# Row maxima of the second attention: the two heads of a step reduced by one VectorE instruction instead of two

## What is computed

```python
x = layernorm(x + differential_attention(x))   # 16 heads of width 8
x = layernorm(x + fp4_ffn(x))                   # 352 hidden
x = layernorm(x + causal_attention(x))          # 16 query heads, 4 key heads, width 64, rotary
x = layernorm(x + top1_experts(x))              # 8 experts, 512 hidden
```

```python
logits = einsum('bqhgd,bkhd->bhgqk', rotary(q), rotary(k)) / sqrt(64)
logits = where(causal, logits, -1e30)
w = softmax(logits)                 # exp(l - max l) / sum
out = einsum('bhgqk,bkhd->bqhgd', w, v) @ Wo + bo
```

## Time and profile before

| | |
|---|---|
| median of 3 runs | 1437.1 us (1436.81 to 1442.52) |
| the profiled execution | 1440.72 us, of which the span that the profile shows is 1438.9 us |
| TensorE busy | 1171.1 us (81%) |
| VectorE busy | 796.9 us (55%) |
| ScalarE busy | 646.9 us (45%) |
| GpSimd busy | 466.6 us (32%) |
| mean granted TensorE clock | 0.863 of full speed |

### The profile page before, as it was taken

One profiled execution on the slowest core, in us unless ns is written; L12 is line 12 of the kernel. 1 busy time (PEld: TensorE's weight loads), 2 busy tenths in 40 slices (PEclk: granted clock), 3 DMA queues, 4 the chain that ended last, 5 costly groups with the idle time before them and its releaser, 6 DMA issues. The chain is left out here.

```text
span 1438.9 us, 18598 instructions
## 1 busy us (share of the span) xinstructions
PE 1171.1 (81%) x6601; PEld 562.6 (39%) x6601; DVE 796.9 (55%) x1852; ACT 646.9 (45%) x1456; POOL 466.6 (32%) x495
## 2 busy tenths in 40 slices
PE   2699745888987769899987769899987698999686
PEld 1112221222454424344454424344454465455454
DVE  4677346772875566563875466563775411765212
ACT  1166512665364226666364226666364233165132
POOL 2000024000898040000898040000887020598000
PEclk7578855979998679999998669999998799999799
DMA  5600030000030000000030000000000000000000
GB/s 144 171 2 1 9 95 1 2 1 9 1 92 6 0 1 1 2 2 15 1 91 6 1 1 1 2 2 8 1 1 1 1 1 1 8 1 1 1 1 8
DMA packets 30923, 24.93 MB, mean 17 GB/s; under 512 B 12328, under 2 KB 27760, under 8 KB 30064
## 3 DMA queue, kind: packets, MB, share of 16 engines
q1 hardware_dynamic: 30832, 23.75, 6.5%
HBM read 16.01 MB, written 7.34 MB: 16 GB/s over the span
## 5 line engine op out<-in xcount | busy, mean ns | idle before, releaser
L717 DVE TENSOR_REDUCE mx<-ps 128x1 f32<-128x512 f32 x512 | 324.2, 684 | 173.0 <-PE ps L1203 171.3
L981 ACT ACTIVATE PROB<-ps 128x512 f32<-128x512 f32 x512 | 274.2, 603 | 206.4 <-PE ps L1194 205.4
L436 POOL TENSOR_SCALAR PROB<-PROB,rsum 128x128 f32<-128x128 f32 (+3 forms) x256 | 278.6, 1105 | 18.1 <-DVE rsum L857 18.0
L1023 ACT ACTIVATE PROB<-ps,mx 128x128 f32<-128x128 f32 (+3 forms) x256 | 132.7, 524 | 162.0 <-DVE mx L852 161.3
L1203 PE MATMUL ps<-kst,qst 24*128 24x512 bf16 x512 | 157.4, 456 | 39.8 <-DVE mx L717 26.6
L945 ACT ACTIVATE MREG<-ps,b_sb 128x512 f32<-128x512 f32 x128 | 88.1, 689 | 179.9 <-PE ps L1131 179.3
L1225 PE MATMUL ps<-PROB,v 128*32 128x512 f32 x1024 | 164.5, 723 | 4.2 <-ACT OREG L990 2.4
L1131 PE MATMUL ps<-xnT,w_sb 128*128 128x512 f32 x256 | 148.0, 680 | 10.1 <-DVE MREG L662 5.6
L1194 PE MATMUL ps<-qst,kst 27*128 27x512 bf16 x512 | 131.0, 417 | 28.8 <-ACT PROB L981 17.6
L1283 PE MATMUL ps<-cst,PROB 128*128 128x128 f32 x640 | 111.6, 296 | 46.1 <-POOL PROB L436 25.3
L417 POOL CAST mparts<-mx 128x16 bf16<-128x16 f32 x32 | 6.3, 196 | 439.1 <-DVE mx L717 439.1
(11 more groups left out here) (182 smaller groups left out, 1317.0 us busy)
## 6 DMA issues: line engine op xcount, KB each, us to landing
qk_terms<-RREG SPq DMA_DIRECT2D x48, 128.0 KB, 2.1
kst<-qk_terms SPq DMA_DIRECT2D x16, 192.0 KB
qst<-qk_terms SPq DMA_DIRECT2D x16, 192.0 KB
w_sb<-in_L_ffn_W_dram SPq DMA_DIRECT2D x1, 2048.0 KB
qst<-mrow SPq DMA_DIRECT2D x96, 4.0 KB
ZC<-in_L_attn_x_dram SPq DMA_DIRECT2D x4, 256.0 KB, 2.9
XN<-in_L_attn_x_dram SPq DMA_DIRECT2D x4, 256.0 KB, 7.9
out_dram<-XP SPq DMA_DIRECT2D x4, 256.0 KB, 2.3
```

What stands on the lines that cost most here:

```text
L436: pool.tensor_scalar(tile, tile, rsum1[:, 2 * v + half:2 * v + half + 1], None, ALU.mult).then_inc(scaled1, 1)
L717: dve.tensor_reduce(mx0[:, ga % 2, col:col + 1], ps[:, max_banks[MAX_SLOT[n] % len(max_banks)], :], AX, ALU.max, negate=True).then_inc(slo ...
L981: act.activation(prob0[:, s % 2, q % 4, q % 8 // 4], ps[:, s0_banks[q % len(s0_banks)], :], ACT.Exp, scale=float(HD0) ** -0.5).then_inc(ex ...
L1023: act.activation(prob1[:, half, at:at + w], ps[:, a1_bank(v, half), 0:w], ACT.Exp, bias=mx1[:, col:col + 1], accum_out=sum1[:, col:col + 1 ...
```

## The change

`maxima(v)` issues one reduction over both heads' banks, which are neighbours, in place of two: the input has three dimensions (128 partitions, 2 banks, `n` keys), the output two columns of `mx1`. It waits once, until both heads' scores are there, and adds one to `max1_done` in place of two. `probabilities(v)` waits for that count once, ahead of the first head's exponential. No instruction changes its place on any engine; 256 reductions become 128.

```diff
                 def maxima(v):
-                    for half in range(2):
-                        col = 2 * v + half
-                        dve.wait_ge(a1_ready, 2 * NV * r + col + 1)
-                        dve.tensor_reduce(mx1[:, col:col + 1], ps[:, a1_bank(v, half), 0:P * (v % 4 + 1)], AX, ALU.max,
-                                          negate=True).then_inc(max1_done, 1)
+                    dve.wait_ge(a1_ready, 2 * (NV * r + v + 1))
+                    banks = ps[:, a1_bank(v, 0):a1_bank(v, 0) + 2, 0:P * (v % 4 + 1)]
+                    dve.tensor_reduce(mx1[:, 2 * v:2 * v + 2], banks, AX, ALU.max, negate=True).then_inc(max1_done, 1)
...
                     for half in range(2):
                         col = 2 * v + half
-                        act.wait_ge(max1_done, 2 * NV * r + col + 1)
+                        if half == 0:
+                            act.wait_ge(max1_done, NV * r + v + 1)
```

## The result

The changed kernel takes 1450.5 us in the median of 5 runs (1448.51 to 1451.02), against 1437.1 us for the kernel before on the same chip (5 runs, 1436.46 to 1442.52). The ratio is 1.0082 with a 95% interval of 1.0062 to 1.0102: slower, by 13.4 us between the medians and by some 12 by the ratio, clear of the 0.5% that can be told from no change, and outside the predicted range.

A forecast was written before the change was run, and what follows sets the result against it. GpSimd's scaling was taken as the limit, VectorE and ScalarE mattering only where it stops for them. Terms -0.1, +0.45 and +0.27 sum to +0.6 us on the 1437.1 median: 1437.7, range 1433.5 to 1443.

The forecast's parts named there:

- The price of the merged instruction: VectorE's merged maximum, interpolated at 416, 684, about 950 and 1213 ns for the four widths; upper bound 1368 at the widest.
- The gain of 0.08 us a step: On VectorE, the merged 512-wide maximum was to be 0.08 us shorter than two maxima in a row, which take 1.29.
- The signal's lag: The merged maximum starts at the second head's score signal, put about 0.07 us behind the first's.
- The steady stops of the last attention: GpSimd's 6 stops before scaling in the last attention: each 0.01 us shorter, about -0.1 us in all.
- ScalarE's copy: Copy of the transposes, behind 384-wide exponentials: 0.40 to 0.47 us late against cover of 0.44; 0 to 0.03 a pair, taken as 0.
- The banks: Score banks released by the 512-wide exponentials: a delay of up to 0.60 us covered by 1.5 us, so 0.
- The table loads: ScalarE's table loads in the first three attentions, without cover: +0.15 us each, +0.45 together.
- the third attention's first loads: First table loads there stand behind 256-wide exponentials, 0.27 us late: +0.27 us; no stop in the two attentions before.
- The slower rival: ScalarE's copy later than its cover in every pair, up to 0.53 us for 32 pairs: 17 us, 1454; chance 8%.

The follow-up runs named there:

- the kernel with one wait: Kernel before, with VectorE waiting for both heads' scores ahead of two separate maxima: 1436.76 us against 1436.65, ratio 0.9998.
- The delayed kernel: Kernel before plus 4, 4, 3 and 2 spare GpSimd multiplications ahead of the last scaling of the four second attentions: 1451.95 us against 1438.43, ratio 1.0101.
- The kernel merged in the narrow steps alone: Kernel before with maxima merged only in the 128- and 256-wide steps: 1441.27 us against 1436.65, ratio 1.0031.
- The kernel with its reciprocals first: Kernel before with VectorE's reciprocals of the previous step issued ahead of the maxima at 512-wide steps: 1444.35 us against 1437.32, ratio 1.0049.

## Why the prediction was wrong

It said 1437.7 us, no change. The time is 1450.5.

- **The price of the merged instruction** was right (1221 ns against 1213). The gain of 0.08 us a step was close: VectorE's busy time fell by 7.9 us over 128 steps, 0.06 each. The weighing of the Trainium skill's page "VectorE: DVE Perf Modes" stands in its result: the pair in the timeline, not the full fixed part, was the measure. But the section "The DRAIN you can't avoid" was read by half: it goes on that a next operation that is not held (made to wait until all earlier ones have finished) starts earlier, and the pair of 1.29 us, 0.08 less than 2 x 684 ns, agrees with that. The signal's lag was put at 0.07 us and is 0.02 to 0.04 us: by the kernel with one wait, and by the merged 512-wide maximum, which starts 0.35 us behind the mask products (1302.30 against 1301.95) instead of 0.31.
- **The steady stops of the last attention** were to change by hundredths: the stop ahead of the 384-wide scaling did (0.41 to 0.38). But from the third pair on a second stop of 0.32 to 0.36 us appeared ahead of the 512-wide scaling, three in all.
- **The step that failed** is "ScalarE's copy: it ends at 1293.55 [...] against a cover of 0.44: 0 to 0.03 a pair, taken as 0". The lateness that one step gives its copy was right, the cover was not. I measured it at one copy and held one step's lateness against it. There are four copies in a pair. TensorE loses 0.13 us at the one of 256 columns, whose exponentials are only 0.13 late. What it loses there makes the next scores, maxima and exponentials late, which adds to what the copy of 512 loses by its own step. In numbers: that copy starts 2.47 us behind the 384-wide step's mask products instead of 2.03 (1299.49 to 1301.96; 1290.94 to 1292.97 before), which is 0.44, as forecast; and these mask products already stand 0.15 later in the pair (1299.49 - 1294.81 = 4.68 us behind the start of its 384-wide scaling, instead of 1290.94 - 1286.41 = 4.53). Together that is 0.59 against a cover of 0.44. And the cover of the narrow scores, some 0.05 us of GpSimd's time ahead of the 512-wide scaling (before, the reciprocals end at 1297.64, and the 384-wide scaling at 1297.78, with 0.10 us from the reciprocals to the next scaling), I did not write down as a term at all. The attentions were to lose 0.6 us and lost 7.7.
- **The banks** had the cover that was claimed: the weight loads of the scores wait for exponentials 5 times for 2.0 us in all, before 16 times for 6.2.
- **The table loads**, the one place with a forecast loss, behaved in kind: stops of 1.03, 1.42 and 0.94 became 1.30, 1.65 and 0.88 us. For each of the first three attentions 0.15 was forecast, and these three stops alone grew by 0.44 in the first. The 0.27 us forecast for the third attention's first loads came as 0.28 (0.87 to 1.15). For the same loads in the first two attentions I wrote "no stop", and there the largest new stops stand, 0.97 and 0.93 us, with TensorE's clock at 0.50. That the clock could fall inside an attention had no term.
- **The slower rival** named the mechanism, the engine and the place, and got 8%. Its price, 17 us, was too high for the attentions (7.7), so that its 1454 lies near the measured 1450.5 is in part luck. Its condition was wrong: it was to need a merged maximum 0.1 us dearer than interpolated. It needed nothing.
- **The stretches between the attentions** had no term. The changed kernel's profile shows 4.8 us more in the first two of them, and a startup, a third stretch and an end that are 4.7 us shorter together. The delayed kernel, with about the same length of the attentions (+8.2 us), costs as much in the median (13.5) as the change (13.4), so a second cost of the change is not needed, though it is not excluded. How the 5.7 us that the change costs beyond its attentions divide up is not shown: one execution of each kernel was profiled, and none of the kernel before near its median. The kernel merged in the narrow steps alone shows how much hangs on that. Its profile differs from that of the kernel before by 0.6 us in the attentions and 0.6 in the time (1441.27 against 1440.72), and yet its median is 4.6 us higher; why is open.

## What to carry to other kernels

Before two small instructions are merged, look at who uses the result of the first while the second runs: a merged instruction gives back a small fixed part (here some 0.07 us) and delays the first consumer by the whole second half, and here the consumer's engine had a copy queued behind it that TensorE waited for. A cover of a few tenths has to be checked at every place in the loop where the late engine is waited for, with the lateness carried around once, and a cover about as large as the lateness is no cover. When a change of one stage moves a kernel by more than that stage, measure a delay of the same size before looking for a second cause, and read the granted clock in short windows wherever a stop is new: the lateness may be small and what the clock does with it large.

## What the hardware showed

Work that starts a few us later or earlier can find TensorE's clock rising 8 us later (62.8 or 71.0 us behind the second attention), which costs about 4 us for each such stretch (219.8 or 224.1 us). The kernel with its reciprocals first gained 2.2 us in the attentions and lost 8.9 in the two stretches between them, and with 2 us of spare work the stretches were back at 219.7 and 219.8. The change itself costs 7.7 us in the attentions, so for an edit of this size the length of the edited stage says more than the total.

The clock can also fall inside a busy stage. Where TensorE stood idle for 1.73 us in place of 1.31, the 16 matmuls behind took 4.07 us in place of 2.38, at a granted clock of 0.50 in place of 1.00.

A reduction over two PSUM banks with one output each costs what a reduction over as many elements of one bank costs: 686 ns for 2 x 256 against 684 for 512, and 421 for 2 x 128 against 416 for 256. From 512 to 1024 elements it is (1221 - 686) / 512 = 1.04 ns an element.
